# Attention scores from three products of rounded halves in place of one full-precision product, with the halves made during the pair before

## What is computed

```
s = jnp.einsum('bthd,bshd->bhts', q, k) * scale
logits = DEG * jnp.log(jnp.abs(s) + 1e-30) + log_G[:, :, :, None] - log_G[:, :, None, :]
m = jax.lax.stop_gradient(jnp.max(logits, axis=-1, keepdims=True))
a = jnp.exp(logits - m)
num = jnp.einsum('bhts,bshd->bthd', a, v)
```

## Time and profile before

| | us |
|---|---|
| median of 3 runs | 2334.22 (2331.72 to 2335.29) |
| profiled execution, its time | 2336.56 |
| profiled execution, its span | 2334.8 |
| busy in the span: PE, DVE, ACT, POOL | 2131.1, 1860.9, 1360.9, 833.5 |

### The profile page before, as it was taken

One profiled execution on the slowest core, in us unless ns is written; L12 is line 12 of the kernel. 1 busy time (PEld: TensorE's weight loads), 2 busy tenths in 40 slices (PEclk: granted clock), 3 DMA queues, 4 the chain that ended last, 5 costly groups with the idle time before them and its releaser, 6 DMA issues. The chain is left out here.

```text
span 2334.8 us, 41518 instructions
## 1 busy us (share of the span) xinstructions
PE 2131.1 (91%) x12373; PEld 1300.3 (56%) x12373; DVE 1860.9 (80%) x2796; ACT 1360.9 (58%) x2399; POOL 833.5 (36%) x785
## 2 busy tenths in 40 slices
PE   6888878999999999999999999699944999999994
PEld 5666652333333333333333333389833899999994
DVE  6888866888888888888888888677858677777773
ACT  4555546666667666676766676344410665666562
POOL 3777751111111111111111111156626565666564
PEclk9999999999999999999999999899965999999997
DMA  4444452221222211222211220234431343444344
GB/s 159 128 127 122 122 149 86 82 52 39 82 77 77 82 46 46 77 82 77 80 50 44 77 82 14 83 111 132 131 128 47 83 85 81 85 84 85 79 84 105
DMA packets 192150, 202.05 MB, mean 87 GB/s; under 512 B 44312, under 2 KB 169440, under 8 KB 185376
## 3 DMA queue, kind: packets, MB, share of 16 engines
q1 hardware_dynamic: 159360, 152.33, 22.3%
q0 software_dynamic: 15840, 22.29, 6.0%
q10 hardware_dynamic: 16768, 25.17, 3.5%
HBM read 128.97 MB, written 74.97 MB: 87 GB/s over the span
## 5 line engine op out<-in xcount | busy, mean ns | idle before, releaser
L851 ACT ACTIVATE att_sb_a<-att_ps_s,att_sb_fg,att_sb_f 128x1024 f32<-128x1024 f32 x384 | 459.4, 1205 | 339.7 <-PE att_ps_s L972 303.1
L887 DVE TENSOR_TENSOR att_sb_acc<-att_sb_acc,att_sb_a 128x1024 f32<-128x1024 f32 (+1 forms) x528 | 534.6, 1040 | 44.3 <-ACT att_sb_a L851 41.9
L810 POOL TENSOR_SCALAR_AFFINE_SELECT att_sb_dec<-att_sb_dec 128x128 f32<-128x128 f32 x256 | 136.0, 531 | 1010.6 <-ACT att_sb_dec L841 1010.6
L972 PE MATMUL att_ps_s<-first_sb_q,first_sb_k 64*128 64x512 f32 (+3 forms) x1280 | 288.5, 557 | 6.5 <-DMA att_sb_hb<-half_log 6.5
L972 PE MATMUL att_ps_s<-att_sb_q,att_sb_k 64*128 64x512 f32 (+3 forms) x1280 | 287.0, 554 | 0.0
L903 DVE SCALAR_TENSOR_TENSOR att_sb_a<-att_ps_s,att_sb_dec 128x1024 f32<-128x1024 f32 (+3 forms) x256 | 209.8, 820 | 84.4 <-PE att_ps_s L972 76.0
L1724 DVE TENSOR_TENSOR ffn_sb_h_lo<-ffn_sb_h,ffn_sb_h_hi 128x256 fp32r<-128x256 f32 x320 | 212.9, 705 | 35.4 <-ACT ffn_sb_h_hi L1612 22.9
L1619 ACT ACTIVATE ffn_sb_h<-ffn_ps_p,ffn_sb_b_cols 128x256 f32<-128x256 f32 x320 | 151.5, 476 | 138.6 <-PE ffn_ps_p L1810 128.6
L972 PEld LDWEIGHTS att_ps_s<-first_sb_q,first_sb_k 64*128 64x128 f32 x1280 | 107.3, 186 | 200.2 <-issue 155.4
L972 PEld LDWEIGHTS att_ps_s<-att_sb_q,att_sb_k 64*128 64x128 f32 x1280 | 106.6, 186 | 191.1 <-issue 152.3
L986 PE MATMUL att_ps_off<-att_sb_a,first_sb_v 128*64 128x512 f32 x768 | 196.2, 600 | 0.2 <-ACT att_sb_a L851 0.2
(11 more groups left out here) (245 smaller groups left out, 4091.4 us busy)
## 6 DMA issues: line engine op xcount, KB each, us to landing
ffn_sb_raw<-L_ffn_W ACTq DMA_DIRECT2D x36, 512.0 KB
close_sb_nT<-num_rows SPq DMA_DIRECT2D x34, 512.0 KB, 4.0
q_rows<-proj_sb_rT SPq DMA_DIRECT2D x64, 256.0 KB, 2.2
att_sb_hb<-half_log SPq DMA_DIRECT2D x16, 1024.0 KB, 14.2
num_rows<-att_sb_num SPq DMA_DIRECT2D x64, 256.0 KB, 2.1
v_cent<-proj_sb_vt SPq DMA_DIRECT2D x32, 256.0 KB, 2.4
k_rows<-proj_sb_rT SPq DMA_DIRECT2D x32, 256.0 KB, 2.4
first_sb_q<-q_rows SPq DMA_DIRECT2D x8, 1024.0 KB, 7.6
```

Source lines behind the costliest of these rows:

```text
L810: nc.gpsimd.affine_select(out=tile, in_=tile, compare_op=ALU.is_ge, fill=0.0, base=0, pattern=[[1, P]], channel_multiplier=-1).then_inc(de ...
L851: nc.scalar.activation(x, s_ps[slot(op)][:, :, :], ACT.Square, scale=f[:, p, i - 1, s:s + 1], bias=fg[:, p, i - 1, s:s + 1]).then_inc(sq_d ...
L887: nc.vector.tensor_tensor(x[:, :, c:TB], x[:, :, c:TB], y[:, :, c:TB], ALU.max).then_inc(max_done, 1)
L972: last = nc.tensor.matmul(s_ps[slot(op)][:, h, c:TB], k_sb[p][at_h, key * P:(key + 1) * P], q_sb[p][at_h, i * TB + c:(i + 1) * TB], start= ...
```

## The change

Scores are now the sum of three matmuls of rounded operands (type F32R): with q = qh + ql and k = kh + kl, where qh and kh are rounded copies ("heads") and ql and kl what is left ("rests"), the products are kh qh, kh ql and kl qh. ACT makes the heads of a pair in eight copies of 128 x 512, POOL the rests in eight subtractions of the same size, written over q and k. For pair 0 this stands ahead of the attention. For pair q+1 the heads stand in ACT's list at places 22, 23.8, 25.5, ... 34.3 of body q, and each rest stands in POOL's list directly ahead of one of the affine selects of blocks 2 and 0. PE now waits for the rests at the start of a pair. To make room, the running maxima share memory with what the modulation kept (`store`).

```diff
+    act_todo += [(q * N + N * (0.50 + 0.04 * c), "cut", (q + 1, c)) for q in range(PAIRS - 1) for c in range(2 * NB)]
...
+            def rest(q, c):
+                t, at = cuts[c][0], slice(cuts[c][1] * TB, (cuts[c][1] + 1) * TB)
+                raw, head = (k_sb, k_hi) if t == 0 else (q_sb, q_hi)
+                pool.wait_ge(cut_hi, q * len(cuts) + c + 1)
+                nc.gpsimd.tensor_tensor(raw[q % 2][:, at].bitcast(F32R), raw[q % 2][:, at], head[q % 2][:, at].bitcast(F32),
+                                        ALU.subtract).then_inc(cut_lo, 1)
+
+            for c in range(len(cuts)):
+                rest(0, c)
+            halfway = {q * len(OWNS) * ST + 4 + c: (q + 1, c) for q in range(PAIRS - 1) for c in range(len(cuts))}
             for n, (q, _, i, j) in enumerate(dec_order):
+                if n in halfway:
+                    rest(*halfway[n])
                 pool.wait_ge(exp_done, n + 1)
...
+            def head(q, c):
+                t, at = cuts[c][0], slice(cuts[c][1] * TB, (cuts[c][1] + 1) * TB)
+                raw, high = (k_sb, k_hi) if t == 0 else (q_sb, q_hi)
+                arrived(act, q)
+                nc.scalar.activation(high[q % 2][:, at], raw[q % 2][:, at], ACT.Copy).then_inc(cut_hi, 1)
+
             arrived(act, 0)
+            for c in range(len(cuts)):
+                head(0, c)
             factors(0)
...
                 if kind == "off" and i == 1 and s == 0:
-                    arrived(pe, q)
+                    pe.wait_ge(cut_lo, (q + 1) * len(cuts))
                 key, c = key_of(op), left(op)
-                for h in range(2):
-                    at_h = slice(h * HD, (h + 1) * HD)
-                    last = nc.tensor.matmul(s_ps[slot(op)][:, h, c:TB], k_sb[p][at_h, key * P:(key + 1) * P],
-                                            q_sb[p][at_h, i * TB + c:(i + 1) * TB], start=True, stop=True)
+                k_lo, q_lo = k_sb[p][:, :].bitcast(F32R), q_sb[p][:, :].bitcast(F32R)
+                terms = ((k_hi[p], q_hi[p]), (k_hi[p], q_lo), (k_lo, q_hi[p]))
+                for n, (left_k, right_q) in enumerate(terms):
+                    for h in range(2):
+                        at_h = slice(h * HD, (h + 1) * HD)
+                        last = nc.tensor.matmul(s_ps[slot(op)][:, h, c:TB], left_k[at_h, key * P:(key + 1) * P],
+                                                right_q[at_h, i * TB + c:(i + 1) * TB], start=(n == 0), stop=(n == len(terms) - 1))
```

More of the change, by code:

```diff
@@ L90, in early_memory, with rows_memory @@
     return early
-def rows_memory(nc, ctx):
+def rows_memory(nc, store):
     rows = Keep()
[L96 to L99, removed]
+    rows.silu = store[:, 0:B * KD * P].rearrange("p (b k t) -> p b k t", b=B, k=KD)
+    rows.w = store[:, B * KD * P:B * KD * P + KD * 6 * D].rearrange("p (k n) -> p k n", k=KD)
+    rows.w_in = nc.alloc_semaphore("rows_w_in")
     return rows
@@ L667, in __iter__, with attend @@
         return iter(self.ops)
-def attend(nc, keep, first, q_rows, k_rows, v_cent, half_log, num_rows):
+def attend(nc, keep, first, store, q_rows, k_rows, v_cent, half_log, num_rows):
     N, place = attention_places()
@@ L764, in attend @@
         a = m.sbuf("a", [P, A, 2, TB])
-        acc = m.sbuf("acc", [P, NB, 2, TB])
+        acc = store[:, :].rearrange("p (i h c) -> p i h c", i=NB, h=2)
+        q_hi = [m.sbuf(f"q_hi{i}", [P, T], F32R) for i in range(2)]
+        k_hi = [m.sbuf(f"k_hi{i}", [P, T], F32R) for i in range(2)]
+        cuts = [(t, c) for c in range(NB) for t in range(2)]
+        cut_hi, cut_lo = m.sem("cut_hi"), m.sem("cut_lo")
         part = m.sbuf("part", [P, 2, TB])
@@ L865, in _ @@
                     query_factor(*op)
+                elif what == "cut":
+                    head(*op)
                 else:
@@ L1990, in build @@
         with ExitStack() as until_attended:
-            rows = rows_memory(nc, until_attended)
+            store = Program(nc, until_attended, "keep").sbuf("store", [P, NB * 2 * TB])
+            rows = rows_memory(nc, store)
             with ExitStack() as until_projected:
@@ L1998, in build @@
             decays(nc, keep, first, rows, used_up, gate_logit, half_log, q_rows, k_rows, v_cent)
-            attend(nc, keep, first, q_rows, k_rows, v_cent, half_log, num_rows)
+            attend(nc, keep, first, store, q_rows, k_rows, v_cent, half_log, num_rows)
         h2_rows = scratch("h2_rows", (NTT, P, D))
```

## The result

The changed kernel takes 2436.61 us (median of 4 runs, 2430.84 to 2439.47) against 2334.42 us for the kernel before, measured beside it: a ratio of 1.0437, interval 1.0413 to 1.046. The forecast was 2366 us with a range of 2312 to 2410. The direction was right, and the time lies above the range.

The account below looks back on a forecast made before the run. PE was taken to bound the attention before, DVE after the change. Terms: 28 for bodies 1 to 14, -2.2 for body 0, -4.2 for body 15, +10.5 for the start: +32, 2366 us, range 2312 to 2410.

Parts of the forecast that it names:

- PE's price of a tile: Scores on PE: three products of 0.235 us, 0.705 a tile of 512 columns against 0.85; 4.2 us saved a body.
- Rival 4: Scores on PE: rounded matmuls of both heads run one after the other, 1.41 us a tile, about 2630 us; chance 0.05.
- ACT's wait and what reaches PE: First head at place 22: ACT stands 6 us for hb, and PE loses 4.0 us a body.
- Rival 2: Bodies: ACT's wait does not reach PE; 2303 us with contention alone, 2277 with neither; chance together 0.15.
- the start: Before the attention: PE's first scores wait for eight heads and eight rests, until 367; +10.5 us in sum.
- the rests: POOL's subtractions beside DVE: each costs DVE 0.8 us, six count, 5 us a body.
- Rival 1: Bodies: load wait without contention from the rests; body 70.1 us, 2334 in all; chance 0.18.
- the sum for a body: Bodies 1 to 14: DVE's chain of 72.3 us exceeds PE's 70.1 and sets the body, 2.0 us more than before.
- DVE's stand at place 23: DVE waits 5.9 us a body for the affine select queued behind the first rest, before its product.
- rival 3: Bodies: strict order couples more, DVE late, then ACT's square, then PE; 75 us a body, 2406 in all; chance 0.12.
- its bound of 77.5: DVE's body with each of eight rests at its full 1.28 us: 61.4 + 10.2 + 5.9.
- the clock: At the start only: PE at half clock after its idle time, up to 1 us more.

Follow-up runs that it names:

- e4_own_loads_tiny: The changed kernel with heads waiting for q and k alone and rests cut to 16 of 512 columns; 2287.61 us, ratio 0.9812.
- e3_tiny_rests: The changed kernel with each rest formed for 16 of its 512 columns, all waits kept; 2362.5 us, ratio 1.0126.
- e1_own_loads: The changed kernel with a semaphore of their own for q and k, heads waiting for these alone; 2366.3 us, ratio 1.0143.
- e5_filled_wait: e3_tiny_rests with four matmuls of zeros added on PE between places 24 and 25 of bodies 1 to 14; 2338.89 us, ratio 1.0027.
- e9_change_filled: The changed kernel, rests in full, with four matmuls of zeros in PE's wait of bodies 1 to 14; 2432.03 us, ratio 1.0409.
- the first four runs: In this 2 x 2: the changed kernel, e1_own_loads, e3_tiny_rests and e4_own_loads_tiny; 2436.6, 2366.3, 2362.5 and 2287.61 us.
- e2_late_cuts: The changed kernel with heads moved to places 29 to 36.4 and rests ahead of the body's last affine selects; 2339.98 us, ratio 1.0022.
- e7_vector_rests: The changed kernel with late heads (places 29 to 36.4) and rests made by DVE 1.5 places behind them; 2314.97 us, ratio 0.9921.

## Why the prediction was wrong

**Right: PE's price of a tile.** In the changed body a tile's products follow each other by 0.23 us (1083.91 to 1084.14), 0.70 a tile, with both heads side by side; e4_own_loads_tiny gives the body, 66.38 against 66.1. Rival 4 is out.

**Right: ACT's wait and what reaches PE.** Forecast 6 us and 4.0. Measured 83.4 / 14 = 6.0 us for ACT (the wait for hb, in 14 bodies) and 4.0 for PE. The first head starts 16.4 us after the first issue in the mean of the 14 bodies (14.9 to 18.2; the body shown above is the latest), where 16.5 was forecast; the body with only this in it, clock kept, is 69.9 at best against 70.1. Rival 2 is out.

**Right: the start.** PE's first scores at 367.10, forecast 367. Up to the issue of the loads of pair 2 the kernel is 10.9 us late. The forecast's terms give 10.5 - 2.2 for the start and body 0, less 4.2 x 15/44 = 1.4 for the first 15 places of body 1, so 6.9: about 4 us of the miss are here. From PE's first scores to that issue it takes 88.2 us, but 82.7 in e3_tiny_rests, where body 0 has no wait for loads either. e4_own_loads_tiny, also with tiny rests but with its first values tile at half clock like the change (1.97 and 1.98 us, against 1.08 in e3_tiny_rests), takes 85.5. So 2.7 us belong to the rests, for which the forecast had 2, and 2.8 to how the attention gets going.

**Right in kind, too large in size: the rests.** Forecast 5 us of DVE's time a body. DVE is busy for 64.9 us a body against 61.4 before, 3.5 more, and the mean of the maxima of 128 x 1024 rose from 1231 ns to 1372. The whole body pays more than that: it changes by 5.6 us between e4_own_loads_tiny and e1_own_loads, 4.2 between e3_tiny_rests and the change, and 5.3 between e5_filled_wait and e9_change_filled. Rival 1 is out.

**Wrong: the sum for a body.** The step reads "61.4 + 5 + 5.9 = 72.3 us, more than PE's 70.1. DVE is now the bound". It took the body to be the longer of two chains, and DVE's chain to have nothing in it but its work and one stand. The trace after, per body:

- DVE busy: 778.56 / 12 = 64.9, forecast 66.4.
- DVE's stand at place 23: 76.5 / 13 = 5.9, forecast 5.9 (13 stands of 4.4 to 7.7 us; the row's fourteenth wait is one of 0.6 us elsewhere).
- DVE's other stands, for PE's transposes, ACT's squares and PE's scores: (36.4 + 28.9 + 10.5) / 13 = 5.8, forecast 0.
- Sum 76.6 of 77.0.

PE's account closes too: 69.5 busy, 4.0 for ACT and 3.5 for DVE make 77.0, where the forecast had 66.1 and 4.0.

DVE's third line is the missing term. The body missed by 77.0 - 72.3 = 4.7 us: 5.8 for these stands, less 1.5 for the rests, and 0.4 that the three lines leave over. Times 14 it is 66 of the 71 us by which the forecast fell short. The two engines do not run as two chains side by side: behind the common stand PE is late for DVE (its transposes, and ACT's squares of its tiles), then DVE, held by the rests, is late for PE, and each such hand-over adds. The stands were there before: from 440 to 1440 us of the kernel before, DVE stands 66.5 + 12.5 us for PE and 36.3 for ACT, nearly all of its 8.9 us of room in a body, which the forecast took as free. And they do not need the long stand at place 23: in e1_own_loads that is down to 28.8 / 12 = 2.4 us a body, where the forecast's step gives 61.4 + 5 + 2.4 = 68.8, but DVE's other stands are (30.3 + 22.3 + 10.4) / 12 = 5.3 and the body is 72.8.

The mechanism is the one that rival 3 names, which had a chance of 0.12. That its bound of 77.5 is where the body came out is luck: the bound books 10.2 us of rests and no other stands, and measured were 3.5 and 5.8. The 2 x 2 of the first four runs shows the same from outside: 67.2 us a body with neither cost, 72.8 with either, 77.0 with both; the full sum would be 78.4, the larger of the two 72.8.

**Wrong, and smaller: the clock.** The forecast saw half clock after idle time at the start, and did not carry it to the new idle time of each body. It is worth 2.1 us a body where PE is the bound (e3_tiny_rests to e5_filled_wait) and some 1.0 or less in the change, as far as the filler brings it back (0.93 to 0.97). By the forecast's own rule it would have brought PE's chain to 70.1 + 2.1 = 72.2 and the body to no more than 72.3; put on top of DVE's chain, to 74.4.

**What stays open.** How the 5.8 us divide between what the common stand leaves behind and what the rests make late: with the stand cut to 2.4 us (e1_own_loads) 5.3 are left, with late heads and no stand (e2_late_cuts) (21.2 + 10.5 + 8.1) / 12 = 3.3, but there the rests lie elsewhere too. Affine selects that stand behind rests are no part of it: apart from place 23, DVE waits for one only once, 0.6 us. They did get longer: from 531.30 to 1455.83 an affine select took 690 ns in the mean (192 of them), against 527 ns in the same bodies of the kernel before, and a rest of q or k 1.6 us against 1.27 at the start, where DVE is idle. Also open is why the landing of hb scatters, from 14.9 to 18.2 us after the first issue.

**Who holds whom.** Rests on POOL raise DVE's busy time by 3.5 us a body in the change and by 66.48 - 61.39 = 5.1 in e2_late_cuts; done by DVE itself they raise it by 65.08 - 61.39 = 3.7. That POOL's side is lengthened too, 1.6 against 1.27 us for a rest, fits what the Trainium skill says in SBUF — State Buffer, section Who interferes with whom: the port pair that the two engines share is an exclusive lock, and the order of issue decides who blocks. The trace agrees, by those two durations.

## What to carry to other kernels

Two costs in a strictly ordered pipeline like this one that fall on different engines are to be summed, not compared, unless the one demonstrably runs in the slack of the other: an engine's slack before a change is made of waits for its neighbours, and these waits remain when it becomes late. Before an operation is put early in a list, read when its data land and what stands behind it, since here the wait at that one place cost 70 us. Work given to GpSimd to relieve VectorE has to be priced at what it holds VectorE for: eight subtractions cost VectorE 3.5 to 5.1 us a body as neighbours, about as much as or more than the 3.7 that they cost as its own.

## What was not expected of the hardware

- In the change each stand of 2.5 to 5.8 us on PE was followed by a mean granted clock of 0.51 to 0.67 over the 10 us from about its end (1.97 us for a values tile, against 1.08). With shorter stands both came out: in e1_own_loads the clock was 1.00 around one of 2.2 us (ending at 535.89) and 0.83 from 550 to 560 around one of 2.0 us (ending at 555.06), and the bodies of e7_vector_rests, with stands of 1.6 and 1.7 us, kept 1.00.
- The affine select of 128 x 128 on POOL, 0.29 us by itself, took 1.28 us where DVE ran maxima of two SBUF operands, as this timeline of POOL and DVE in the changed kernel shows (in the kernel before, too, some took 1.07 to 1.11):

```profile
1099.75 1.88 POOL L815 TENSOR_TENSOR first_sb_q<-first_sb_q,att_sb_q_hi 128x512 fp32r<-128x512 f32 x1 [2.74 <-ACT att_sb_q_hi L877]
1101.58 1.28 POOL L826 TENSOR_SCALAR_AFFINE_SELECT att_sb_dec<-att_sb_dec 128x128 f32<-128x128 f32 x1
1102.83 1.28 POOL L815 TENSOR_TENSOR first_sb_k<-first_sb_k,att_sb_k_hi 128x512 fp32r<-128x512 f32 x1
...
1099.28 3.42 DVE L913 TENSOR_TENSOR keep_sb_store<-keep_sb_store,att_sb_a 128x1024 f32<-128x1024 f32 x2
```

  Two maxima took 3.42 us here where two of 1.2 would take 2.4, beside a rest of 1.88 us that takes 1.27 alone: the hold goes both ways.
- Rounded tiles of 128 columns for both heads followed each other by 0.06 and 0.12 us (from 1102.93 to 1102.99 and 1103.11), so the first two terms of such a tile took 0.18 us where the forecast had allowed 0.13 for each.
